# GpSimd's two differences of a gated layer in two operations of 256 columns each, with a new sequence of steps on all engines

## The reference, cut to what matters

```
x = layernorm(x + L0(x, adj)); x = layernorm(x + L1(x, adj)); x = layernorm(x + L2(x, adj))
x = layernorm(x + L3(x, adj))

# L3, for each of 5 layers l, with A = (adj != 0):
m   = h @ weight[l];  agg = A^T @ m
r   = sigmoid(agg-gate_r + h-gate_r);  z = sigmoid(agg-gate_z + h-gate_z)
n   = tanh(agg-gate_n + r * h-gate_n)
h   = (1 - z) * n + z * h
```

## Time and profile before

| what | us |
|---|---|
| median of 3 runs | 1662.55 |
| lowest, highest run | 1661.5, 1663.69 |
| the profiled execution's own time | 1665.81 |
| its span in the trace | 1663.4 |
| PE busy | 1575.9 (95%) |
| DVE busy | 1423.2 (86%) |
| ACT busy | 1235.1 (74%) |
| POOL busy | 872.9 (52%) |

### The profile page before, as it was taken

The page is one execution under the profiler, slowest core; times in us unless marked ns, Lnnn a source line. Parts: engine busy times, 40 slices in busy tenths (PEclk is TensorE's granted clock), DMA queues, the critical chain, the costliest instruction groups (busy, mean ns, idle before and its releaser), DMA issues.

```text
span 1663.4 us, 34267 instructions
## 1 busy us (share of the span) xinstructions
PE 1575.9 (95%) x12166; PEld 1263.8 (76%) x12166; DVE 1423.2 (86%) x3696; ACT 1235.1 (74%) x3015; POOL 872.9 (52%) x1006
## 2 busy tenths in 40 slices
PE   8789999999999999999999999999999999999987
PEld 7667787787878778787877878788787877877766
DVE  5687989989898898989989898998979889798776
ACT  3567778786877778787877878787787776877655
...
PEclk9999999999999999999999999999999999999999
...
GB/s 95 20 43 1 31 27 30 14 14 43 14 30 27 18 27 14 43 14 30 25 20 26 14 33 24 30 14 29 28 14 30 27 18 26 14 27 14 14 0 20
DMA packets 84801, 40.88 MB, mean 25 GB/s; under 512 B 10757, under 2 KB 84634, under 8 KB 84634
## 3 DMA queue, kind: packets, MB, share of 16 engines
...
q10 hardware_dynamic: 576, 0.15, 0.0%
...
## 4 chain that ended last, share of the span: by engine, by line
PE 60%; DVE 23%; ACT 8%; POOL 4%; issue 4%; SPq 1%; DMA 0%; POOLq 0%; DVEq 0%; ACTq 0%
PE RA L1092 14%; PE RB L1092 13%; PE Q L1052 6%; PE RT L1052 4%; DVE stats L786 3%; PE Q L1203 3%; PE Q L1220 2%; DVE tr L958 2%; DVE un L953 2%; ACT e_s L704 2%; PE M L1131 2%; DVE s_ng L892 2%; DVE p_s L901 1%; ACT nn L744 1%; PE RT L1286 1%
## 5 line engine op out<-in xcount | busy, mean ns | idle before, releaser
L704 ACT ACTIVATE e_s<-Q,s_ng 128x128 f32<-128x128 f32 x1024 | 291.7, 392 | 27.1 <-DVE s_ng L892 26.9
L622 POOL TENSOR_TENSOR h_lo<-hT,h_hi 128x512 fp32r<-128x512 f32 (+1 forms) x163 | 204.8, 1257 | 155.8 <-ACT h_hi L730 127.0
L630 POOL TENSOR_TENSOR hd<-hT,nn 128x512 f32<-128x512 f32 x156 | 201.5, 1292 | 134.7 <-ACT nn L744 134.1
L626 POOL TENSOR_SCALAR un<-tr 128x512 f32<-128x512 f32 (+1 forms) x164 | 104.1, 635 | 294.7 <-ACT tr L740 294.6
L744 ACT ACTIVATE nn<-tr,wT 128x512 f32<-128x512 f32 (+1 forms) x164 | 118.0, 722 | 81.9 <-DVE tr L958 80.6
L892 DVE TENSOR_REDUCE s_ng<-Q 128x4 f32<-128x512 f32 x256 | 168.6, 681 | 8.7 <-PE Q L1203 8.4
L901 DVE TENSOR_TENSOR p_s<-Q,adjTe 128x512 f32<-128x512 f32 x256 | 169.4, 683 | 5.5 <-PE Q L1052 4.6
L740 ACT ACTIVATE tr<-RA,b_rz 128x512 f32<-128x512 f32 (+1 forms) x160 | 111.0, 694 | 73.2 <-PE RA L1092 71.9
L1052 PE MATMUL Q<-ident,e_s 128*128 128x128 f32 x1024 | 153.0, 277 | 7.3 <-ACT e_s L704 7.2
L1092 PE MATMUL RA<-agg_hi,comp_hi 128*128 128x512 f32 (+1 forms) x320 | 145.7, 455 | 11.0 <-DVE agg_lo L943 10.2
L1052 PEld LDWEIGHTS Q<-ident,e_s 128*128 128x128 f32 x1024 | 123.8, 143 | 35.8 <-ACT e_s L704 15.1
...
## 6 DMA issues: line engine op xcount, KB each, us to landing
...
```

The lines of the kernel that those rows point to most:

```text
L622: pool.tensor_tensor(h_lo[g][:, c], hT[g][:, c], h_hi[g][:, c], ALU.subtract).then_inc(SG["h_lo"][g], 1)
L630: pool.tensor_tensor(hd[g][:, c], hT[g][:, c], nn[g][:, c], ALU.subtract).then_inc(SG["hd"][g], 1)
L704: ins = act.activation(e_s[:, j, c, :], Q[j][:, c * P:(c + 1) * P], ACT.Exp, bias=s_ng[:, j, c:c + 1])
```

## The change

In `steps` of GpSimd both differences are issued as two operations, each over one half of the columns; only the second one sets the semaphore. A tile of 512 columns becomes 256 and 256. Where a part has 256 columns (the last group from layer 1 on) it becomes 128 and 128.

```diff
+            def halves(c):
+
+                first = c.start or 0
+                last = W if c.stop is None else c.stop
+                middle = (first + last) // 2
+                return slice(first, middle), slice(middle, last)
...
-                        pool.tensor_tensor(h_lo[g][:, c], hT[g][:, c], h_hi[g][:, c], ALU.subtract).then_inc(SG["h_lo"][g], 1)
+                        for h in halves(c):
+                            ins = pool.tensor_tensor(h_lo[g][:, h], hT[g][:, h], h_hi[g][:, h], ALU.subtract)
+                        ins.then_inc(SG["h_lo"][g], 1)
...
-                        pool.tensor_tensor(hd[g][:, c], hT[g][:, c], nn[g][:, c], ALU.subtract).then_inc(SG["hd"][g], 1)
+                        for h in halves(c):
+                            ins = pool.tensor_tensor(hd[g][:, h], hT[g][:, h], nn[g][:, h], ALU.subtract)
+                        ins.then_inc(SG["hd"][g], 1)
```

The twelve strings of `MERGE` are replaced. Their lengths and the steps in them stay the same (2176 steps on TensorE, 2059 on VectorE, 1470 on ScalarE, 751 on GpSimd); 1113, 1114, 923 and 356 of these keep their place. The mean shift of a step is below 1.1 places on each engine, the largest 14, 32, 6 and 15 places. First row of each string:

```diff
-    tensor=(("ABBBBABBBBBBBAABBAABAAABAABAABABAABABAABABABABAAAABABAABAABATAATAAARARRIAZZBABTAABTARBRARIAZZBABATBBTAARRRABBA"
+    tensor=(("BAABBABBBBBBBAABBBAABAABAABAABBAAABBAAABABABABAAAABABABAAABATAATARAARARIAZZBAATBATBRABRRAIAZZBBATBBATARRARBATI"
...
-    vector=(("CCBBBBCBBBBBCBMMMMBPPBPPBCBBMMBMMBPPPPCAAAAACMMMMPRPPPBMMMMPCCPPRPCARAAACBABRCBRRMMMMRRPBBPPRCRPCCRBRMBMMBRRSM"
+    vector=(("CBBCBCBBBBCBBBMMMMPPBPPCBBBBMMBMBMPPPPCRAAAAAMMMMCPPPPBMMMMPCPCPRPCAAARACBRASBCRRMMMMBRRBPPRBPCRCPBCRBRMBBRRMM"
...
```

More of the change, by code:

```diff
@@ L69 @@
-    vector=(("CCBBBBCBBBBBCBMMMMBPPBPPBCBBMMBMMBPPPPCAAAAACMMMMPRPPPBMMMMPCCPPRPCARAAACBABRCBRRMMMMRRPBBPPRCRPCCRBRMBMMBRRSM"
[L70 to L94, removed]
+    tensor=(("BAABBABBBBBBBAABBBAABAABAABAABBAAABBAAABABABABAAAABABABAAABATAATARAARARIAZZBAATBATBRABRRAIAZZBBATBBATARRARBATI"
+             "BAAZBATAARZARRTAIZZTABRRBRTAIZTBZARRARITABATZZBRRRATBIATZZARRARTBAAIZATZATAARARTARBIATZZARRBATARITZZRABRRTIATZ"
+             "ZBRRBARIATBZAZTRBBRATRAIBAABZTZABATARBRRATIAZTZRABRRAITABAZZTARRARTIZBATZBRRRTIABZTAZBRRATRAAAZITZATAARARARTIB"
+             "ZTZARRBARTAIZTBZRABRARTAIZTZRBRRABTIAZZTABRBARTABRAABIATZZAATBARRTABRITZAZARRABRTIZAZBTRARRTIABZTZBRRTRITAZZAA"
+             "BRATRABRAATIAAZZ"),
+            ("TARARTRATIZZABRRABRITABAZZBTRARRTAIZTZRBRRBIATAZZTBBARRARTABBAAIBAZTAATZARRTRATIBZAAZRRABRTIBZATZRARTARITBZAZB"
+             "RRATRIAZTZRRARTBAIAAZBZTAA"),
+            ("TARATRARITBZZRRBRTIBZAATZARARRBATIATZZRRRBTIAZZABTRABBATRARIAABZZATBAATRBATBRRTIAZZBRRRAITAAZZATBARRTARITBZAZB"
+             "RRTBARITZZARRARTAZAABITZAAATARTRATRIBZZRRARATBIZATZABRRRBTIATZZARRRTIABZTAZARBRABRTABZAABBIAZTAATBRARTARTIBZAZ"
+             "BARRRTIBZTAZARRRATIABTZZBRRTRABAIZATZARRTABRAAIATAZTRZRARATIAZTZRBARRATABIZABTZBRRRTIAZTAZBRRRAITBAAZZTRBBRART"
+             "ABBAIAZBATBZAATRARRTIATZBZRRBRITAZAATAZRARTRATIZZBARRRATBIZATZRRATBARBAAZAITATAZRATRARIBAZTZABRRARTIBAZZTRBART"
+             "ARITZZARRRTAIZTAAZRRRTAZIAAZATAATARRTRIATZZRRRATIBZTAZARRARTAIATZZBRRTARAIZTAZARRTARIAAZATZATRRTRITZZRRRBTIZTZ"
+             "BRRRTIZTZRRRTIZZTRRTIRTTZZRRRTITZZRRRTIZZTRRRTIZTZRRRTIZTZRRRIZZTTTRRRIZZTTRRRIZZT")),
@@ new lines @@
+    vector=(("CBBCBCBBBBCBBBMMMMPPBPPCBBBBMMBMBMPPPPCRAAAAAMMMMCPPPPBMMMMPCPCPRPCAAARACBRASBCRRMMMMBRRBPPRBPCRCPBCRBRMMBRRMM"
+             "SRPSPRPCPRAAAARASRCRSMRSMMPRMSSRSRPSRPRPSBRSMMRMSSCRSRPPMSRPRCPRRSRCAAAARRSCASRSCBMSMRRMMSPBRBRPBPRSPSCRSBSBCR"
+             "SRMBMSCRMRBSMSRPPPRSSPSSSARAASRASCSRARSRSMMMRSPMSPRRSPPSRCRMSBSRMMPRSMSCRSRPCPSRRPRRRSCARAAASRCABRSCSMMRSRMBMS"
+             "BPRBRBPSBRPSCRPCSSCRSRMBSMRBRMMSSRPPPRSSPSSSAAASARCRSASRRCRMMMSSPRMSSPRSRPPSRRBSSRMMMMRSSCSRRPCSPRRPPRRRRCARAA"
+             "ASSCASS"),
+            ("BRCBBSRMMRSBMBPRBRMPSCSRPPCRSSCRSRBMSMBRMRSSRPMPRPSSPSSAASSAARRSCARSRCRSMMSMRMPSSRSRPPPSRRBRMSSMMMPRSSCRSRPPSC"
+             "RRPSRSAARRAACSSRRCA"),
+            ("BRCBSMRRMBBSMMRRBSCRSCPPRPSPSCRSRBMSBRRMSMSBMRPPSSRPPSSRSASRASAACARRSRCSSMRMMSMSPRPRSPPSRRBRMSSMMMPRSSCSRRCSPP"
+             "RRPSRRRACSRAAACRSABRSCSMMRRMBBSMBRRPPSBRSCRSPSPBRSCRCSRMRBMSRMSMPBRPPSSPRSSSSAAAACSRARRSRMMSSMMPRSSCRSRPPSPRRS"
+             "BRSMMMRMSSCCRSRPPPSRRPRRSRRAAAARBSCARCCSSBRBSRMBMMBSRBRMPPSBRSCRSSPPRSCRCSMRMRMBSMSPRPRSPSPSRSSSRAASAACARSRCRS"
+             "SMMRMMSSRRSPPPPSRRRSMMSBMRMSSPPRSRCSRCRPPRRSAARAARCSRCASRSCSMMRRMMPSRRPCSSRPPCSRSCSMRRMSMRRMPSRSCPRPSSPRSSSSAA"
+             "AASRASRRCRSSMMRSSMRSRPMPSPRRPSRSMMRMMSSCRSRPPPSRRPRRRSRAAAASRASRSCSRRSRRSRSRSSRSRSRRSSRCSRSSSRRSSSSRSRSSRRSSRR"
+             "SRSRSSRSRSRSSRSSSSSSSSSSSSSSSS")),
@@ new lines @@
+    scalar=(("BBBBBBDAAMMMDMAMMMMBBAABAABBMMMMBACMCMMMDRARARARARMRMCMRCRMDRARRMBMRMRMBSRABSARASRASRMSSRMBRMSBMSRRSBRASCRMSCR"
+             "MSMRSRMDSARRASRASRARSMMSRCRMSMRCRSSADRSRSMRMSMRSBRSMBRASBSARSRSASARBSMRSMRMBMSRRSASBMRSCRSCRMSMDRSRMSARRARSASR"
+             "ARSMRSCRMSMMRCRDSSARSRSRMMSMRBSMRSBARSASBRRASSASRMBMRSMSRMSBRRSBASRSCMRSCRSMSRMRMSDARRASRS"),
+            ("ARARSSMRRMCMSCMRDSRSARSSRRMSMBMRSRSMBRABSARSASSRASRMMSRMSBRBMSRSRBASRMRSCMSCRMSMRSRSDASRSARR"),
+            ("ARASRMSRCMRSCRMDMRSSRASRSRSMRMSSMBRMRABSRASRBASSARBSRSMSMRMBMSRSRBASRMRSCMSCRSDMSRRMSARSSARARRASRSMMRMRCSMRCSR"
+             "SDRSARSRSMRMMRSSMBRABSBASARRSSARSMMRBSMSBRMSRSRSBARSCRMSCMRSMMRSRSDARARRRSSRAASRMSRMCMSMRCSDRSRSASRRMSMMRBSMRS"
+             "BRABSASRRASSASBRRSBMSRMMSMRSRBASRMSRSCMRMSCRSRMSDARASRRASRASRMMRCSRMCSMRDSSRARSMSRRMSMRMSRSRASARSASSRASRSRSMRM"
+             "SMRSMRSRACSRMSCMRSMMRSRSARSARSRRRSSRRSCRSRSRSCRSRSRSSRRSSSRRSRSRSRSRSRSRRSSRSRSRSSSSSSSSSSSSSS")),
@@ new lines @@
+    gpsimd=(("BDDBDAADAAACCDDRBARCARRDRCDRRARSRAASRSRSRSCRASRCSRDSRDRSACARSBRSRSRSRSDCRSRADSSRASRASRSRSCRSRCSRSDRADRSABRCASR"
+             "SRSDRASRDSRSCSRSARSACARSRSRSSRRSCRDSRDSRA"),
+            ("BRCSARSRSDRSRSCRSRADSRSASCRASRSRSRSRSRSCDARSDRA"),
+            ("BRCSRSARSDRSRSCRSDARSRSASCARSRSRSRSRSARSDCRDSRABARCSRSRSRSRDSRSRACDSSRSARASRSRCSSRRSARDCSRRDASBRCASRSRSRSARSRS"
+             "CDDRSSRAAASRSRCSRSRSRSRSCRDDRSACARSRSRSDARSDRCSRSRSRSASCARSRSRSRSRSCRSARSRARCSRSRSRSRSRSCRSRSSRSRSRSRRSSRSSSSS"
```

## The result

The kernel after took 1664.03 us in the median of 20 runs (1660.75 to 1666.94), the kernel before 1662.45 us in 20 runs beside them (1658.2 to 1666.01). The ratio is 1.0013 [1.0007, 1.0019]: slower by 1 to 3 us, inside my range, on the other side of a forecast of 0.4 us less.

The account below looks back on a forecast made before the run. PE bounds the kernel, busy 1575.9 of 1663.4 us, so only its waits can move. Terms 0.5 + 0.5 + 0 - 0.4 - 1 = -0.4 us gave 1662.2 us, range 1653 to 1672 us.

Parts of the forecast that it names:

- GpSimd's cost: Pairs of halves on GpSimd take longer than whole operations: 45 us more busy time, to about 918 us.
- the 0 for it: PE's r of group 0, layer 2, behind h_lo: two more B steps ahead cover the longer pair, costing 0.
- 2.2 more: DVE's 16 waits for hd, at 0.14 us each: 2.2 us of DVE, counted as 0.5 us of the total.
- The relief at the pass end: L804's fourth operation ends 0.54 us earlier between the halves; 0.2 us a pass left in the old order, 0.4 us counted.
- "0" for the new sequence: New order of steps: pass end zero, PE's gaps elsewhere set against each other as 0, with 0.4 us a pass either way.
- Start and end: Start and drain: almost nothing, 0.5 us for the drain; a difference over 4 us would make the forecast wrong.
- Rival 2: Lock handed over between halves and used by the new order: faster by 7 us, 1655.5 us; chance 0.32.
- Rival 3: DVE gets in between the halves and delays h_lo: slower by 7 us, 1669.5 us; chance 0.16.
- Rival 4: Narrow gaps of the new order, z2 to turn, stall PE: slower by 4 us, 1666.6 us; chance 0.14.
- A pass above 98.1: Sign in the pass length, expected 97.3 to 98.0 us: above 98.1, rival 3 or 4 holds, told apart by PE's waits.
- The 1.22 us: Sign at the pass end: the chain's stretch of waiting for nothing visible shrinks from 1.22 to below 0.7 us.
- L804 without durations above 1 us under `h_lo`: Sign on DVE: no such long L804 operations; staying near 1.3 us would mean GpSimd keeps the lock between halves.

Follow-up runs that it names:

- e10: e3 with hd whole again, so only h_lo in halves: 1648.72 us, 0.9931 of the kernel before.
- e3: The changed kernel with the old order for passes 5 to 12, new order kept for start and drain: 1649.97 us, 0.9923 of the kernel before.
- e11: e3 with h_lo whole again, so only hd in halves: 1652.71 us, 0.9955 of the kernel before.
- e7: The changed kernel with GpSimd's x2d moved behind h_lo of layer 3 in passes 5 to 12: 1659.25 us, 0.9983 of the kernel before.
- e6: The changed kernel with VectorE's h_new of the pass end back behind wo in passes 5 to 12: 1661.61 us, 0.9996 of the kernel before.
- e1: The kernel before with only the halves added, old order everywhere: 1659.71 us, 0.9987 of the kernel before.
- e4: The kernel before, whole tiles, with the new order for start and drain only: 1653.31 us, 0.9946 of the kernel before.

## Why the prediction was wrong

**GpSimd's cost: right.** 45 us of pairs, measured 44.6. POOL came to 925.3 and not 918. The other 7 us are a net sum: `rs`, `un`, `ve` and the roots of the degrees grew by 1.9 to 2.6 us each, `ve` and `rs` under VectorE at the pass end as shown; `x1b` fell by 4.5 us. PE's wait for `h_lo` rose by 0.3 us in all, which bears out the 0 for it. DVE's wait for `hd` grew from 8.0 to 14.9 us where I had 2.2 more; with the old passes the halves of `hd` alone make 2.8 (8.3 in e10, 11.1 in e3), and cost no time.

**The relief at the pass end: right in mechanism, too small.** "0.2 us a pass in the old order" was 0.26 at that place and 0.4 a pass (97.67 to 97.3; 97.63 to 97.23 in e11 and e10). In the old order `x1` came 0.54 us earlier to PE, the whole of what I had for it. I had added a short wait of GpSimd's second half for L804, and there was none.

**"0" for the new sequence: the step that failed.** Measured are +1.46 us a pass, +8.8 us over eight passes in the traces, and -5.7 and -6.2 us for start and end; over whole runs +10.4 to +14 and -9. Of the +1.46 us, 0.93 and 0.66 lie at places 2 and 1, 0.38 at a third that stays open, and -0.5 elsewhere. Three mistakes lie in the 0:

- *Place 2 wasn't looked at* (+0.93 us a pass, the largest). I wrote out the order of the pass end and "set against each other" the gaps elsewhere, by PE's order only. The lock sits between VectorE and GpSimd, so it was their two strings that had to be laid side by side: ten columns moved by three steps met `x2d`. The rule that I had weighed (Trainium skill, "SBUF — State Buffer", "Who interferes with whom": the blocked side waits for the whole instruction) gives this price, and the 0.98 us of ten columns agree with it. e7 shows the cause: 0.82 of the 0.93 us go with the neighbour.
- *The pass end* (+0.66 us ahead of `x1_t`). I followed `h_new` ahead of `x1` as 0.69 us of DVE and then let `h_lo` catch the *last* operation of `x1`. It also holds up GpSimd's `rs`, on which `x1` depends, so the *first* one is caught and two of four are. e6 shows `h_new`'s part, 0.5 of the 0.66 us (the rest is not shown); it also shows that putting it back buys little, since `qkv` takes half of that.
- *Start and end* (-12 us in the traces). I left both at almost nothing (0.5 us for the drain) and said that over 4 us there would make the forecast wrong. That they nearly cancel the longer passes is luck, and it is why the total missed by 2 us only. Which steps of these strings bring it, no run here tells.

**The rivals.** Rival 2 (the lock is handed over, faster) holds with the old passes, at a third to a half of its price: e1 is 2.5 us faster, and e3 is 3.3 faster than e4, where it had 7, since `h_lo` is next in line, as I had objected. With the new order it did not come. Rival 3 (DVE gets in between the halves and delays `h_lo`) fell: the halves keep 735 and 739 ns, and the waits for `h_lo` stay at 2.2 us. Rival 4 (narrow gaps) is wrong for `z2` to `turn`: PE's wait for `hT` is 5.0 us before and after. For `agg` to `r2` it may be right, 0.38 us a pass, but two tries at its cause missed and it stays open.

**The signs that I named.** A pass above 98.1 was to mean rival 3 or 4, told apart by PE's waits for `h_lo` and `hT`. The pass was 99.13 and neither wait had moved by more than 0.3 us. Both signs came from my own list of mechanisms; sorting all of PE's waits by how much they had grown would have named `h_rem` at once. The 1.22 us of "issue" in the chain shrank to 0.68 us at the same place, below my 0.7, and said nothing about the time either. L804 without durations above 1 us under `h_lo` came true: the longest `x<-xin` is 0.895 us, 1.451 before. View of L815 in after:

```profile
L815 DVE TENSOR_SCALAR x<-xin,mv,rs x128: 332/340/895, 31.5 to 1505.8; 128x128 f32<-128x128 f32 x128
```

That a symptom goes and the time grows all the same is the lesson of this case: one long block had become two short ones, 0.81 + 0.76 for 1.35 us.
